# Last stage of a ViT layer: sums kept in three buffers of their own, and loads issued in front of stores

## Chip, cores and metric

One core of a Trainium2 chip. The metric is the device time of one launch in microseconds (us), the median of several runs. In names of the text a number in brackets is a block or a chunk: combine(23), low(29).

## What is computed

A patch embedding, a long convolution along the tokens and a mixture-of-experts layer over 64 images of 197 tokens with 192 channels. What matters here is the end of the last line:

```python
gates, idx = jax.lax.top_k(probs, TOPK_ROUTED)        # 2 of 8 experts
routed = jnp.einsum('bse,bsed->bsd', dense_g, expert_out)
shared = jax.nn.silu(x @ ws_gate) * (x @ ws_up) @ ws_down
return alpha * shared + (1.0 - alpha) * routed         # and h + this
```

For each token the result is a residual row plus `alpha` times the shared expert's row, plus one row from each of its two experts. The latter two rows ("parts") were scattered to DRAM by the stage before.

## The kernel before

The 12,608 tokens are 25 blocks (`NBLK`) of 512, the last one with 384. An earlier stage computes the shared expert of blocks 0 to 19 (`NOW` = 20); the routed experts follow; `finish` (from L1888) is the last stage, and the only one the change touches. It does two things side by side:

- **The shared expert of blocks 20 to 24**, in 30 chunks c = 0 to 29, six for a block (128 of 768 hidden columns each). PE does `up(c)` (gate and up products, L1969), then `down(c - 2)` (L1986). ACT applies SiLU (L2004) and casts the hidden values to `hh` (L2011). DVE does `hidden(c)` (L2029, one input in PSUM, the other in SBUF) and `low(c - 1)` (L2035, `hl` = `hf` minus `hh`, both inputs in SBUF). After a block's last chunk DVE adds PE's rows to `sums` (`token_out`, L2042).
- **The final sum and store of all 25 blocks.** SP loads the two parts of a block into `y[b % 5]` (`load(b)`, L1934); POOL adds them (L2019); DVE adds the block's `sums` (`combine(b)`, L2057, in place in `y`); SP stores the result to the images (`store(b)`, L1945).

Each engine works its list in order. DVE's list is written in the loop at the end of `vector`: in chunk c it issues hidden(c), low(c - 1), after each sixth chunk token_out, and from c = 6 on combine(c - 6). combine(23) falls into the last chunk; low(29), the last token_out and combine(24) follow. So whatever combine(b) waits for also holds hidden(b + 7), behind it, and with it ACT and PE.

SP's list is the loop in `sync`. `RING` = 5 buffers `y`, but `BEHIND` = 3: ahead of load(b) stands store(b - 3), which waits until combine(b - 3) is done, and load(b) itself waits until store(b - 5), the one that emptied its buffer, has landed. `xt` is a ring of 8 buffers (`XR`) with transposed rows for PE, 1,536 values of 16 bits per partition each; the last stage reads those of blocks 20 to 24, which are `xt[4]` to `xt[7]` and `xt[0]`.

Of the kernel before, what the change touches and what calls it, by code (L numbers as in the profile page):

```python
# [14 lines left out]
F32 = mybir.dt.float32  # L15
F16 = mybir.dt.float16
U32 = mybir.dt.uint32
ALU = mybir.AluOpType
ACT = mybir.ActivationFunctionType

B, C, IMG, P = 64, 3, 224, 16
# [4 lines left out]
D = 192  # L26
# [34 lines left out]
BT, NT = 512, 4  # L61
LAST_NT = 3
NBLK = NTOK // BT + 1
CLASS_TILE = LAST_NT - 1
# [21 lines left out]
NOW = NBLK - NLATE  # L86
PACE = [5, 5, 4] * ((NBLK - 1) // 3) + [8]
XR = 8
# [118 lines left out]
def embed(nc, io, outer, u, area, taps, pairs, resid, cls, consts, early_in, corners, row_out, yc, uc, k0, spare, weights):  # L207

    with ExitStack() as ctx:
# [318 lines left out]
        def vector(dve):  # L528
# [193 lines left out]
            for at in range(NG + 2):  # L722
                if 0 < at < NG:
                    fold(at)
                    if at % QG == 0:
                        low_rows(at // QG)
                chain(at)
                if 0 <= at - 2:
                    finish(at - 2)
# [173 lines left out]
def feed_forward(nc, io, embedded, mixing, sums, row_out, weights, resid, cls, routed, parts, out, consts):  # L903

    with ExitStack() as ctx:
# [11 lines left out]
        shared = shared_expert(nc, io, ctx, sems, t, mixing, row_out, weights, resid, cls, routed, out, consts)  # L917
        experts = routed_experts(nc, ctx, sems, t, weights, routed, parts)
        end = finish(nc, ctx, sems, t, weights, parts, out)
        block = ctx.enter_context(nc.Block())  # L920

# [45 lines left out]
def tiles(b):  # L967
    return NT if b < NBLK - 1 else LAST_NT if b == NBLK - 1 else 0


def shared_weights(t):

    w = t["w"]
    wa = [x[:, 0:2 * HS].rearrange("p (k h) -> p k h", k=2) for x in w]
    wb = [x[:, 2 * HS:4 * HS].rearrange("p (k h) -> p k h", k=2) for x in w]
    wd = [x[:, 4 * HS:W_SHARED].rearrange("p (m d) -> p m d", m=NSH) for x in w]
    return wa, wb, wd


def patch_tiles(b):  # L980
    return NT if b < NBLK - 1 else CLASS_TILE


def tile_sums(t, b, i):

    if b == NBLK - 1 and i == CLASS_TILE:
        return halves(t["class"][:])
    at = (b * NT + i) * DH
    return t["sums"][:, :, at:at + DH]


def block_sums(t, b):

    at = b * NT * DH
    return t["sums"][:, :, at:at + patch_tiles(b) * DH].rearrange("p k (t d) -> p k t d", d=DH)


def halves(row):
    return row.rearrange("p (k d) -> p k d", k=2)


def tile_halves(rows):
    return rows.rearrange("p t (k d) -> p k t d", k=2)
# [877 lines left out]
def finish(nc, outer, sems, t, weights, parts, out):  # L1881

    with ExitStack() as ctx:
        def sb(name, shape, dt=F32):
            return ctx.enter_context(nc.sbuf_tensor("end_" + name, shape, dt))

        def sem(name):
            return outer.enter_context(nc.semaphore("e_" + name))  # L1888

        RING, BEHIND = 5, 3  # L1890
        wa, wb, wd = shared_weights(t)
        xt, alpha = t["xt"], t["alpha"]
        y = [sb(f"part{i}", [128, 2, NT, D]) for i in range(3)]
        sb("gap", [128, 584])
        sg = [weights["stage"][0][:, i * BT:(i + 1) * BT] for i in range(2)]
        hf = [weights["stage"][1][:, i * BT:(i + 1) * BT] for i in range(2)]
        hh = [sb(f"hh{i}", [128, BT], F16) for i in range(2)]
# [4 lines left out]
        ctx.enter_context(nc.psum_tensor("end_unused", [128, 2, 512], F32))  # L1902
        pso = ctx.enter_context(nc.psum_tensor("end_out", [128, 2, 512], F32))
        y_in = [sem(f"y_in{i}") for i in range(RING)]
        stored = [sem(f"stored{i}") for i in range(BEHIND)]
        pair_added, all_added = sem("pair_added"), sem("all_added")
        g_ps, u_ps, sg_ready, hf_ready, hh_ready, hl_ready, down_ps, out_ready = (
            sems[n] for n in ("g_ps", "u_ps", "sg_ready", "hf_ready", "hh_ready", "hl_ready", "down", "out_ready"))
# [4 lines left out]
        def place(c):  # L1913

            j, m = divmod(c, NSH)
            return NOW + j, m, tiles(NOW + j)

        LAST = NBLK - 1
        CLASS_ROW = LAST * BT + CLASS_TILE * 128

        def sync(sp, rounds):
            for q in range(RL):
                sp.wait_ge(sems[f"r_sent{q}"], 64 * rounds + 64 * (STRAIGHT // RY))
            sp.wait_ge(sems["r_turn"], 64 * rounds + 64 * (STRAIGHT // RY))
            for q in range(RL, RY):
                sp.wait_ge(sems[f"r_sent{q}"], 64 * (STRAIGHT // RY))

            images = out[0:NTOK].rearrange("(b l) d -> b l d", l=SEQ)

            def load(b):  # L1930
                i, n = b % RING, patch_tiles(b)
                for k in range(2):
                    at = k * NTOK + b * BT
                    sp.dma_start(y[i][:, k, 0:n], parts[at:at + n * 128].rearrange("(p t) d -> p t d", t=n)  # L1934
                                 ).then_inc(y_in[i], 16)
                    if b == LAST:
                        at = k * NTOK + CLASS_ROW
                        sp.dma_start(y[i][0:B, k, CLASS_TILE], parts[at:at + B]).then_inc(y_in[i], 16)

            def store(b):  # L1940
                sp.wait_ge(all_added, b + 1)
                i, n = b % RING, patch_tiles(b)
                for half in range(2):
                    at = 1 + half * HALF + b * NT
                    sp.dma_start(images[:, at:at + n], y[i][half * B:(half + 1) * B, 0, 0:n]).then_inc(stored[b % BEHIND], 16)  # L1945
                if b == LAST:
                    sp.dma_start(images[:, 0], y[i][0:B, 0, CLASS_TILE]).then_inc(stored[b % BEHIND], 16)

            for b in range(NBLK):
                if b >= BEHIND:  # L1950
                    store(b - BEHIND)
                if b >= RING:
                    sp.wait_ge(stored[(b - RING) % BEHIND], 32 * ((b - RING) // BEHIND + 1))
                load(b)
            for b in range(NBLK - BEHIND, NBLK):
                store(b)
            for i in range(BEHIND):
                sp.wait_ge(stored[i], 32 * len(range(i, NBLK, BEHIND)) + (16 if i == LAST % BEHIND else 0))

        def tensor(pe, rounds):  # L1960
            def up(c):
# [60 lines left out]
        def vector(dve):  # L2022
            def hidden(c):
                i, n = c % 2, place(c)[2] * 128
                dve.wait_ge(sg_ready, DONE + c + 1)
                dve.wait_ge(u_ps, DONE + c + 1)
                if c >= 2:
                    dve.wait_ge(hl_ready, DONE + c - 1)
                nc.vector.scalar_tensor_tensor(out=hf[i][:, 0:n], in0=psu[:, i, 0:n], scalar=1.0 / SCALE,  # L2029
                                               in1=sg[i][:, 0:n], op0=ALU.mult, op1=ALU.mult).then_inc(hf_ready, 1)  # L2030

            def low(c):
                i, n = c % 2, place(c)[2] * 128
                dve.wait_ge(hh_ready, DONE + c + 1)
                nc.vector.tensor_tensor(hl[i][:, 0:n], hf[i][:, 0:n], hh[i][:, 0:n],  # L2035
                                        ALU.subtract).then_inc(hl_ready, 1)

            def token_out(b):
                dve.wait_ge(down_ps, NSH * (b + 1))
                for i in range(tiles(b)):  # L2040
                    sums = tile_sums(t, b, i)
                    last = nc.vector.scalar_tensor_tensor(  # L2042
                        out=sums, in0=halves(pso[:, i // 2, (i % 2) * D:(i % 2 + 1) * D]),
                        scalar=alpha[b % XR][:, i:i + 1], in1=sums, op0=ALU.mult, op1=ALU.add)
                    if i % 2 or i == tiles(b) - 1:
                        last.then_inc(out_ready, 1)

            def combine(b):
                i = b % RING
                dve.wait_ge(pair_added, b + 1)  # L2050
                if b >= NOW:
                    dve.wait_ge(out_ready, 2 * (b + 1))
                n = patch_tiles(b)
                if b == LAST:
                    nc.vector.tensor_tensor(y[i][0:B, 0, n], t["class"][0:B], y[i][0:B, 0, n], ALU.add)
                total = tile_halves(y[i][:, 0, 0:n])
                nc.vector.tensor_tensor(total, block_sums(t, b), total, ALU.add).then_inc(all_added, 1)  # L2057

            done = 0
            for c in range(CHUNKS):  # L2060
                hidden(c)
                if c:
                    low(c - 1)
                if c % NSH == 1 and c > NSH:
                    token_out(NOW + c // NSH - 1)
                while done < c + 1 - FIRST_COMBINED:
                    combine(done)
                    done += 1
            low(CHUNKS - 1)
            token_out(NBLK - 1)  # L2070
            for b in range(done, NBLK):
                combine(b)

        return {"sync": sync, "tensor": tensor, "scalar": scalar, "gpsimd": gpsimd, "vector": vector}


# [138 lines left out]
```

## Time and profile before

| what | us |
|---|---|
| median of 3 runs | 1130.31 (1129.49 to 1130.46) |
| the profiled execution's own time | 1131.53 |
| its span in the trace | 1129.5 |
| last stage, from PE's first product (L1969) to the end of the span | 1006.5 to 1129.5 |

The span is what the trace's clock covers; times inside it count from its start. The profiled execution took 1131.53 us, of which 2.0 us lie outside the span. The stages before 1006 us are the same code before and after the change. Start from a DVE row, see what its bracket says it idled for, and go from there to POOL's and SP's rows.

### The profile page before, as it was taken

Reading aid. Unit: us, or ns where it says so; the run is one execution under the profiler, and the core shown is the slowest. Engines: PE = TensorE matmul, PEld = TensorE weight load, DVE = VectorE, ACT = ScalarE, POOL = GpSimd, SP = SyncE. Lnnn points to the kernel's source line nnn. Section 1 sums busy time; section 2 is a strip of 40 time slices with the busy share of each in tenths; the row PEclk is TensorE's granted clock in tenths of the full one; section 3 lists DMA queues with packets and bytes.
Section 4 is the critical chain, followed back from the end, with each engine's and each line's share of the span. In section 5 each row is a group of like instructions: output and inputs, shape, how many; then the busy total and the mean of one; then the engine's idle time right before and its main releaser. Section 6 shows DMA issues by size and latency. Waiting matters only on the chain.

```text
span 1129.5 us, 24252 instructions
## 1 busy us (share of the span) xinstructions
PE 1022.7 (91%) x7867; PEld 715.8 (63%) x7868; DVE 890.9 (79%) x2663; ACT 557.7 (49%) x1047; POOL 630.2 (56%) x637
## 2 busy tenths in 40 slices
PE   5969899599499999999999999899999999989884
PEld 4968788589366666666666666556666656656452
DVE  6999967567688888988888886678888888866885
ACT  1134534357655565565555555246565656543231
POOL 0134521200367777777777786237777777773453
PEclk9999999789699999999999999999999999999898
DMA  9596687866422323332222233747676767616896
GB/s 330 201 306 214 203 284 238 194 173 164 122 72 65 117 69 118 115 96 88 73 82 68 70 105 118 217 96 156 146 163 139 160 146 165 148 66 219 293 316 212
DMA packets 192772, 178.64 MB, mean 158 GB/s; under 512 B 127050, under 2 KB 156942, under 8 KB 192650
## 3 DMA queue, kind: packets, MB, share of 16 engines
q1 hardware_dynamic: 158402, 127.47, 41.3%
q0 software_dynamic: 19488, 39.17, 9.9%
q10 hardware_dynamic: 14760, 10.46, 2.9%
q8 instruction: 67, 1.10, 0.4%
q14 instruction: 55, 0.45, 0.1%
HBM read 90.78 MB, written 66.93 MB: 140 GB/s over the span
## 4 chain that ended last, share of the span: by engine, by line
PE 44%; POOL 19%; DVE 16%; issue 15%; DMA 3%; ACT 1%; SPq 1%; POOLq 0%; ACTq 0%; DVEq 0%
POOL routed L1378 13%; PE u_out L1747 7%; PE ps L514 6%; PE u_gate L1731 5%; PE u_short L1731 5%; PE u_up L1731 5%; PE conv L816 4%; DMA end_part<-parts 3%; DVE u L538 2%; POOL rs L1354 2%; DVE sums L644 2%; PE psg L1212 2%; PE conv L820 2%; PE pso L1227 2%; PE psu L1212 2%
## 5 line engine op out<-in xcount | busy, mean ns | idle before, releaser
L1807 POOL DMA_INDIRECT parts<-unit_yu,unit_token x208 | 204.6, 984 | 89.7 <-issue 49.4
L1378 POOL DMA_INDIRECT routed<-rows_w,slot x198 | 215.1, 1086 | 64.6 <-issue 64.3
L514 PE MATMUL ps<-w,sums 128*98 128x192 f32 x768 | 148.0, 338 | 5.2 <-DVE sums L644 5.2
L1559 DVE SCALAR_TENSOR_TENSOR hf<-psu,sg 128x512 f32<-128x512 f32 x120 | 82.8, 690 | 66.2 <-PE psu L1212 42.5
L1299 ACT ACTIVATE sg<-psg 128x512 f32<-128x512 f32 x120 | 71.9, 599 | 126.8 <-PE psg L1212 126.7
L1227 PE MATMUL pso<-ffn_w_hi,hh 128*128 128x192 f16 x480 | 119.0, 248 | 13.0 <-DVE hl L1564 9.9
L514 PEld LDWEIGHTS ps<-w,sums 128*98 128x98 f32 x768 | 121.9, 170 | 13.3 <-DVE sums L644 5.5
L445 POOL TENSOR_TENSOR e_rs<-e_ve,mhalf 98x8 f32<-98x8 f32 x16 | 50.5, 3154 | 140.0 <-DVE e_ve L681 133.2
L1227 PE MATMUL pso<-ffn_w_hi,hl 128*128 128x192 f16 x480 | 119.0, 248 | 0.0
L1227 PE MATMUL pso<-ffn_w_lo,hh 128*128 128x192 f16 x480 | 118.9, 248 | 0.0
L1212 PE MATMUL psg<-xt,ffn_w_hi 128*128 128x512 f16 x360 | 118.2, 383 | 0.0
L1212 PE MATMUL psu<-xt,ffn_w_hi 128*128 128x512 f16 x360 | 117.2, 380 | 0.0
L393 ACT ACTIVATE u<-sums,e_nb,e_rs 98x192 f32<-98x192 f32 x124 | 56.1, 534 | 90.7 <-POOL e_nb L447 82.1
L1212 PE MATMUL psg<-xt,ffn_w_lo 128*128 128x512 f16 x240 | 91.8, 382 | 0.0
L1212 PE MATMUL psu<-xt,ffn_w_lo 128*128 128x512 f16 x240 | 91.2, 380 | 0.0
L1564 DVE TENSOR_TENSOR hl<-hf,hh 128x512 f16<-128x512 f32 x120 | 90.9, 758 | 0.3 <-ACT hh L1305 0.3
L1772 ACT ACTIVATE unit_yu<-u_out,unit_gates 128x192 f32<-128x192 f32 x104 | 38.1, 418 | 86.2 <-DVE unit_gates L1842 83.3
L1305 ACT CAST hh<-hf 128x512 f16<-128x512 f32 x120 | 73.6, 614 | 8.1 <-DVE hf L1559 7.1
L2019 POOL TENSOR_TENSOR end_part<-end_part 128x768 f32<-128x768 f32 (+1 forms) x25 | 47.9, 1917 | 52.3 <-DMA end_part<-parts 52.3
L1227 PEld LDWEIGHTS pso<-ffn_w_hi,hh 128*128 128x128 f16 x480 | 47.2, 98 | 28.3 <-DVE hl L1564 16.9
L1212 PEld LDWEIGHTS psu<-xt,ffn_w_hi 128*128 128x128 f16 x360 | 35.4, 98 | 43.0 <-issue 0.8
L1860 DVE SCALAR_TENSOR_TENSOR unit_h<-u_up,stage 128x512 f32<-128x512 f32 x52 | 35.9, 691 | 30.2 <-ACT stage L1778 26.9
(236 smaller groups left out, 2768.9 us busy)
## 6 DMA issues: line engine op xcount, KB each, us to landing
sums<-in_xa_dram SPq DMA_DIRECT2D x48, 392.0 KB, 5.5
sums<-in_xb_dram SPq DMA_DIRECT2D x48, 392.0 KB, 6.9
end_part<-parts SPq DMA_DIRECT2D x48, 384.0 KB, 5.1
resid<-sums ACTq DMA_DIRECT2D x32, 294.0 KB
hin<-resid SPq DMA_DIRECT2D x48, 192.0 KB, 3.8
out_dram<-end_part SPq DMA_DIRECT2D x48, 192.0 KB, 3.6
stage<-in_w_all_dram SPq DMA_DIRECT2D x8, 576.0 KB, 4.2
routed<-stage SPq DMA_DIRECT2D x11, 392.0 KB, 5.7
```

Of the source, the lines that this page charges most:

```text
L393: last = nc.scalar.activation(u[0:HALF, n % 2, GI * g + n // 2], h[g % NH][:, n // 2, n % 2], ACT.Identity, bias=nb[g % NH][:, n], scale=r ...
L514: nc.tensor.matmul(out, xa[(C * g + c) % NSLOT][:, t], w32[:, c], start=(plain and c == 0 and k == 0), stop=False, skip_group_check=True)
L1212: last = nc.tensor.matmul(ps[:, m % 2], wt[:, k, cols], xt[b % XR][:, x], start=(a == 0), stop=(a == 4))
L1227: last = nc.tensor.matmul(o, hx[m % 2][:, ts], wd[k][:, m], start=(a == 0 and m == 0 and t % 2 == 0), stop=(a == 2 and m == NSH - 1), skip ...
L1299: nc.scalar.activation(sg[c % 2][:], psg[:, c % 2], ACT.Silu, scale=1.0 / SCALE).then_inc(s["sg_ready"], 1)
L1305: nc.scalar.copy(hh[c % 2][:], hf[c % 2][:]).then_inc(s["hh_ready"], 1)
L1378: nc.gpsimd.indirect_dma_start(out=routed[:, :], out_offset=bass.IndirectOffsetOnAxis(ap=slot[q][:, k, t:t + 1], axis=0), in_=rows_w[q][:, ...
L1559: nc.vector.scalar_tensor_tensor(out=hf[i][:], in0=psu[:, i], scalar=1.0 / SCALE, in1=sg[i][:], op0=ALU.mult, op1=ALU.mult).then_inc(s["hf ...
L1564: nc.vector.tensor_tensor(hl[c % 2][:], hf[c % 2][:], hh[c % 2][:], ALU.subtract).then_inc(s["hl_ready"], 1)
L1731: last = nc.tensor.matmul(ps[:], w[part][:, bass.ds(col + off, 128)], x[:, c], start=(m == 0), stop=(m == 4))
L1747: last = nc.tensor.matmul(o, h[q][:, k * 128:(k + 1) * 128], w[part][:, bass.ds(col + off, D)], start=(m == 0 and k % 2 == 0), stop=(m == ...
L1807: nc.gpsimd.indirect_dma_start(out=parts[:, :], out_offset=bass.IndirectOffsetOnAxis(ap=token[r][:, k:k + 1], axis=0), in_=y[r][:, k, :], ...
```

## The change

```diff
-        RING, BEHIND = 5, 3
+        RING, OUT = 5, 3
+        total = [t["xt"][b % XR][:].rearrange("p c n -> p (c n)").bitcast(F32)[:, 0:NT * D].rearrange("p (t d) -> p t d", t=NT)
+                 for b in range(NOW - OUT, NOW)]
...
             def store(b):
-                sp.wait_ge(all_added, b + 1)
-                i, n = b % RING, patch_tiles(b)
+                i, n = b % OUT, patch_tiles(b)
                 for half in range(2):
                     at = 1 + half * HALF + b * NT
-                    sp.dma_start(images[:, at:at + n], y[i][half * B:(half + 1) * B, 0, 0:n]).then_inc(stored[b % BEHIND], 16)
+                    sp.dma_start(images[:, at:at + n], total[i][half * B:(half + 1) * B, 0:n]).then_inc(stored[i], 16)
...
-            for b in range(NBLK):
-                if b >= BEHIND:
-                    store(b - BEHIND)
+            for b in range(NBLK + RING):
                 if b >= RING:
-                    sp.wait_ge(stored[(b - RING) % BEHIND], 32 * ((b - RING) // BEHIND + 1))
-                load(b)
-            for b in range(NBLK - BEHIND, NBLK):
-                store(b)
+                    sp.wait_ge(all_added, b - RING + 1)
+                if b < NBLK:
+                    load(b)
+                if b >= RING:
+                    store(b - RING)
...
-                n = patch_tiles(b)
+                n, o = patch_tiles(b), total[b % OUT]
+                if b >= OUT:
+                    dve.wait_ge(stored[b % OUT], 32 * (b // OUT))
                 if b == LAST:
-                    nc.vector.tensor_tensor(y[i][0:B, 0, n], t["class"][0:B], y[i][0:B, 0, n], ALU.add)
-                total = tile_halves(y[i][:, 0, 0:n])
-                nc.vector.tensor_tensor(total, block_sums(t, b), total, ALU.add).then_inc(all_added, 1)
+                    nc.vector.tensor_tensor(o[0:B, n], t["class"][0:B], y[i][0:B, 0, n], ALU.add)
+                nc.vector.tensor_tensor(tile_halves(o[:, 0:n]), block_sums(t, b), tile_halves(y[i][:, 0, 0:n]),
+                                        ALU.add).then_inc(all_added, 1)
```

combine(b) now reads `y[b % 5]` and writes `total[b % 3]`, which is `xt[1]`, `xt[2]` or `xt[3]`, last read for blocks 17 to 19. `y[b % 5]` is free once combine(b) is done; the new wait on DVE is for store(b - 3) to have landed, since it reads the same `total`. Sizes and counts of all operations stay.

SP, from the first load of the last stage on. `end_part` is `y`, `xt` is `total`, `out_dram` the images; L1934 (before) and L1936 (changed) are loads, L1945 and L1946 stores. Before:

```order
L1934 DMA end_part<-parts 128x768 [waits r_turn,r_sent3,r_sent4,r_sent2,r_sent5,r_sent1,r_sent0]
L1934 DMA end_part<-parts 128x768 x5
L1945 DMA out_dram<-end_part 64x768 [waits e_all_added]
L1945 DMA out_dram<-end_part 64x768
L1934 DMA end_part<-parts 128x768 x2
L1945 DMA out_dram<-end_part 64x768 [waits e_all_added]
L1945 DMA out_dram<-end_part 64x768
L1934 DMA end_part<-parts 128x768 x2
L1945 DMA out_dram<-end_part 64x768 [waits e_all_added]
L1945 DMA out_dram<-end_part 64x768
L1934 DMA end_part<-parts 128x768 [waits e_stored0]
L1934 DMA end_part<-parts 128x768
```

Changed:

```order
L1936 DMA end_part<-parts 128x768 [waits r_turn,r_sent3,r_sent4,r_sent2,r_sent5,r_sent1,r_sent0]
L1936 DMA end_part<-parts 128x768 x9
L1936 DMA end_part<-parts 128x768 [waits e_all_added]
L1936 DMA end_part<-parts 128x768
L1946 DMA out_dram<-xt 64x768 x2
L1936 DMA end_part<-parts 128x768 [waits e_all_added]
L1936 DMA end_part<-parts 128x768
L1946 DMA out_dram<-xt 64x768 x2
```

Ten loads (five blocks) in place of six go out at once, and a block's stores stand behind the load of the block five later.

DVE, two chunks in the middle of the stage, before:

```order
L2029 SCALAR_TENSOR_TENSOR stage<-end_up,stage 128x512 [waits hl_ready,u_ps,sg_ready]
L2035 TENSOR_TENSOR end_hl<-stage,end_hh 128x512 [waits hh_ready]
L2057 TENSOR_TENSOR end_part<-sums,end_part 128x2x4x96 [waits e_pair_added]
L2029 SCALAR_TENSOR_TENSOR stage<-end_up,stage 128x512 [waits hl_ready,u_ps,sg_ready]
L2035 TENSOR_TENSOR end_hl<-stage,end_hh 128x512 [waits hh_ready]
```

Changed:

```order
L2029 SCALAR_TENSOR_TENSOR stage<-end_up,stage 128x512 [waits hl_ready,u_ps,sg_ready]
L2035 TENSOR_TENSOR end_hl<-stage,end_hh 128x512 [waits hh_ready]
L2058 TENSOR_TENSOR xt<-sums,end_part 128x2x4x96 [waits e_stored2,e_pair_added]
L2029 SCALAR_TENSOR_TENSOR stage<-end_up,stage 128x512 [waits hl_ready,u_ps,sg_ready]
L2035 TENSOR_TENSOR end_hl<-stage,end_hh 128x512 [waits hh_ready]
```

The order of DVE's work is the same; from combine(3) on, combine has one wait more (`e_stored`).

## Rows read from the trace of the kernel before

**Rows 1.** The chain that ended last, 1096 to 1130 us: start, us, what.

```profile
1096.07 0.88 DVE end_part L2057
...
1096.96 0.47 SPq L1945
...
1097.48 0.60 SPq L1945
...
1098.12 0.58 SPq L1934
...
1098.75 6.22 DMA end_part<-parts
...
1105.04 1.82 POOL end_part L2019
...
1106.88 0.97 DVE end_part L2057
```

**Rows 2.** Waits of 1000 to 1130 us: total us, times, longest.

```profile
POOL end_part L2019 <- DMA end_part<-parts: 52.3, 23, 6.5
...
DVE stage L2029 <- PE end_up L1969: 16.2, 10, 2.8
DVE end_part L2057 <- POOL end_part L2019: 12.7, 6, 3.2
```

**Rows 3.** DVE in order of time: start, us, instruction, idle before it.

```profile
1015.19 0.68 DVE L2035 TENSOR_TENSOR end_hl<-stage,end_hh 128x512 f16<-128x512 f32 x1
...
1027.17 0.69 DVE L2029 SCALAR_TENSOR_TENSOR stage<-end_up,stage 128x512 f32<-128x512 f32 x1 [1.86 <-PE end_up L1969]
...
1028.38 2.56 DVE L2057 TENSOR_TENSOR end_part<-sums,end_part 128x768 f32<-128x768 f32 x1
...
1036.46 0.94 DVE L2057 TENSOR_TENSOR end_part<-sums,end_part 128x768 f32<-128x768 f32 x1
...
1050.39 1.69 DVE L2035 TENSOR_TENSOR end_hl<-stage,end_hh 128x512 f16<-128x512 f32 x1
...
1068.37 1.50 DVE L2035 TENSOR_TENSOR end_hl<-stage,end_hh 128x512 f16<-128x512 f32 x1
...
1100.42 0.54 DVE L2035 TENSOR_TENSOR end_hl<-stage,end_hh 128x384 f16<-128x384 f32 x1
...
1117.66 0.96 DVE L2057 TENSOR_TENSOR end_part<-sums,end_part 128x768 f32<-128x768 f32 x1 [2.71 <-POOL end_part L2019]
1118.54 1.89 DVE L2035 TENSOR_TENSOR end_hl<-stage,end_hh 128x384 f16<-128x384 f32 x1
```

**Rows 4.** POOL in order of time, the same columns.

```profile
1049.52 2.02 POOL L2019 TENSOR_TENSOR end_part<-end_part 128x768 f32<-128x768 f32 x1 [1.07 <-DMA end_part<-parts]
...
1093.72 1.80 POOL L2019 TENSOR_TENSOR end_part<-end_part 128x768 f32<-128x768 f32 x1 [1.36 <-DMA end_part<-parts]
```

**Rows 5.** DVE by group and shape, 1004 to 1130 us: xcount | busy us, mean ns | idle.

```profile
L2035 DVE TENSOR_TENSOR end_hl<-stage,end_hh 128x512 f16<-128x512 f32 x24 | 31.3, 1305 | 0.0
L2057 DVE TENSOR_TENSOR end_part<-sums,end_part 128x768 f32<-128x768 f32 x24 | 25.9, 1079 | 12.7 <-POOL end_part L2019 12.7
...
L2035 DVE TENSOR_TENSOR end_hl<-stage,end_hh 128x384 f16<-128x384 f32 x6 | 7.2, 1199 | 0.0
```

**Rows 6.** Windows: busy by engine, granted clock, DMA share, GB/s.

```profile
1030.00:1033.00 3.00, 3.00 (x24) 1.87 (x21) 3.00 (x3) 0.95 (x3) 2.62 (x2) 1.00 0.30 60
1060.00:1063.00 3.00, 0.87 (x7) 0.38 (x6) 3.00 (x4) 0.70 (x2) 1.80 (x1) 1.00 0.62 143
...
1051.00:1054.00 3.00, 3.00 (x10) 1.11 (x9) 1.95 (x2) 1.10 (x2) 0.55 (x2) 0.56 0.95 311
...
1075.00:1115.00 40.00, 31.86 (x230) 19.74 (x228) 34.89 (x43) 11.78 (x23) 21.32 (x11) 1.00 0.96 321
```

**Rows 7.** DMA issues of 1005 to 1130 us: KB each, median us to landing.

```profile
end_part<-parts SPq DMA_DIRECT2D x48, 384.0 KB, 5.1
out_dram<-end_part SPq DMA_DIRECT2D x48, 192.0 KB, 3.6
...
out_dram<-end_part SPq DMA_DIRECT2D x1, 48.0 KB, 2.0
```

**Rows 8.** All stores (L1945): duration of the issue, and us to landing.

```profile
DMA to landing us min/median/max: 2.1/3.5/6.5
```

More of the change, by code:

```diff
@@ L1904, in finish @@
         y_in = [sem(f"y_in{i}") for i in range(RING)]
-        stored = [sem(f"stored{i}") for i in range(BEHIND)]
+        stored = [sem(f"stored{i}") for i in range(OUT)]
         pair_added, all_added = sem("pair_added"), sem("all_added")
@@ L1940, in store @@
             def store(b):
-                sp.wait_ge(all_added, b + 1)
-                i, n = b % RING, patch_tiles(b)
+                i, n = b % OUT, patch_tiles(b)
                 for half in range(2):
                     at = 1 + half * HALF + b * NT
-                    sp.dma_start(images[:, at:at + n], y[i][half * B:(half + 1) * B, 0, 0:n]).then_inc(stored[b % BEHIND], 16)
+                    sp.dma_start(images[:, at:at + n], total[i][half * B:(half + 1) * B, 0:n]).then_inc(stored[i], 16)
                 if b == LAST:
-                    sp.dma_start(images[:, 0], y[i][0:B, 0, CLASS_TILE]).then_inc(stored[b % BEHIND], 16)
-            for b in range(NBLK):
-                if b >= BEHIND:
-                    store(b - BEHIND)
+                    sp.dma_start(images[:, 0], total[i][0:B, CLASS_TILE]).then_inc(stored[i], 16)
+            for b in range(NBLK + RING):
                 if b >= RING:
-                    sp.wait_ge(stored[(b - RING) % BEHIND], 32 * ((b - RING) // BEHIND + 1))
-                load(b)
-            for b in range(NBLK - BEHIND, NBLK):
-                store(b)
-            for i in range(BEHIND):
-                sp.wait_ge(stored[i], 32 * len(range(i, NBLK, BEHIND)) + (16 if i == LAST % BEHIND else 0))
+                    sp.wait_ge(all_added, b - RING + 1)
[3 more added lines that the diff above has]
+                    store(b - RING)
+            for i in range(OUT):
+                sp.wait_ge(stored[i], 32 * len(range(i, NBLK, OUT)) + (16 if i == LAST % OUT else 0))
         def tensor(pe, rounds):
```

## Prediction

> **What bounds the last stage.** The chain that ended last comes first, since every other stage is untouched. At 1096 to 1107 us it reads [rows 1]: combine, two store issues, one load issue, 6.22 us of load, POOL's add, combine. So it walks round a loop: combine(b) is done, SP issues store(b), behind it load(b + 3), and that load is what combine(b + 3) waits for. The list of waits gives the size [rows 2]: DVE idled 12.7 us in 6 waits of combine for POOL's add, and POOL had waited for loads. Ten waits of hidden for PE cost 16.2 us. Those up to 1027.17 us (2.84, 1.47, 0.83 and four of 1.86, in DVE's rows in order of time; the last is in [rows 3]) lie ahead of the first combine and sum to 12.6; the 3.6 left follow such stalls. The granted clock shows why: PE stood still behind a waiting DVE, and 1051 to 1054 us was granted 0.56, mostly the lower level of 1.2 GHz, where most of the stage has 1.00, which is 2.4 GHz [rows 6].
>
> From the start of combine(0), 1028.38, to the end of combine(23), 1118.54 [rows 3], are 90.2 us. DVE idled 12.7 + 3.6 = 16.3 of them and was occupied for the rest. It is the engine that sets the end; from combine(23) to the end of the span is a tail of 11.0 us.
>
> Part of DVE's occupied time is no work. A low takes 0.68 us alone and 1.69 at 1050.39, where POOL's add ran from 1049.52 to 1051.54 [rows 3, 4]: it ends 0.5 us behind POOL's add. By groups [rows 5], with 0.68, 0.54 and 0.94 as the times alone [rows 3], this costs 31.3 - 24 x 0.68 = 15.0, 7.2 - 6 x 0.54 = 4.0 and 25.9 - 24 x 0.94 = 3.3, together 22.3 us. DVE's rows in order of time hold 16 lows over 1.4 us and 2 combines over 2.4: 18 of POOL's 25 adds, 22.3 / 18 = **1.24 us for each add that meets DVE**. The other seven are block 0's and the six for which DVE was waiting idle.
>
> The DMA engines are the third bound, and close: from 1075 to 1115 us they were busy 0.96 at 321 GB/s [rows 6], but earlier there were holes (0.30 at 1030 to 1033, 0.62 at 1060 to 1063).
>
> **The change, part by part.**
>
> *Loads leave two combines earlier.* load(b) waited, through the store ahead of it, for combine(b - 3); now for combine(b - 5). Two chunks are 2 x (90.2 / 23) = 7.8 us, and DVE's longest wait for POOL is 3.2 [rows 2], so all six waits can go: **-12.7 us**. With them go the stalls of PE and what followed them at 1.2 GHz: **-3.6 us**.
>
> *POOL's adds meet DVE.* Six adds ran while DVE stood idle. Now DVE is at work then, so each costs what the others do: 6 x 1.24 = **+7.4 us**. The add of block 24 met low(29) in the tail (1.89 against 0.54 [rows 3], 1.35 us); its load now follows combine(19), so it meets an earlier instruction: 1.35 less in the tail, 1.24 more ahead of it, nothing in the sum. From 0.8 us, the least of the 18 (the low of 1.50 at 1068.37 [rows 3]), to the whole length of an add, 1.80 [rows 4], the six are worth 4.9 to 10.8.
>
> Here a rule speaks against the change. The Trainium skill's page "SBUF — State Buffer" (Who interferes with whom) says that a DVE instruction with two SBUF inputs and a GpSimd instruction that reads SBUF exclude each other for the whole instruction, the loser blocking fully. The trace agrees: the low at 1050.39 ends only after POOL's add has, and hidden, with one input in SBUF, keeps its 0.69. What it would make of an add that always blocks from its start is the second rival below.
>
> *The new wait for store(b - 3).* It can only bite if that store takes longer than three chunks. Between the end of combine(b - 3) and the start of combine(b) lie about 3 x 3.5 - 0.9 = 9.6 us (3.5 is 90.2 less the net 8.9 gained so far, over 23). Before the store stand two load issues (2 x 0.60), then its own two; landing took 3.5 us in the median and 6.5 at most [rows 8]. That is 2.4 + 3.5 to 6.5 = 5.9 to 8.9: hidden, but narrowly, and I cost it at nothing. Its cover is the 0.7 us between 8.9 and 9.6. If the load that now stands ahead of it makes it later by its whole 786 KB, 2.4 us at 321 GB/s, 1.7 are left over in every third combine: 8 x 1.7 = 13.6, the upper end; the lower is zero.
>
> *What the DMA engines allow.* combine(23) needs store(20) landed, and SP asks for all loads ahead of that store: 24 x 786 KB, 492 KB for block 24, and 21 stores of 393 KB (from [rows 7]), 27.6 MB. At the 321 GB/s of the busiest stretch that is 86.0 us, at 321 / 0.96 = 334 it is 82.7. From the first load at 1021.0, with 2.0 us for landing [rows 7] and 0.9 for combine, combine(23) ends no earlier than 1109.9, or 1106.6. DVE's own sum gives 1118.5 - 8.9 = 1109.6. Two bounds meet, and where they do neither is reached. For that meeting no row gives a price. It lies between nothing and 8.9 (all the gain); I take one wait of the size seen now, 12.7 / 6 = **+2.1 us**, near the lower end because the loads have five blocks of slack at the start.
>
> *The rest.* SP issues the same 103 DMAs and drops a wait on its queue; its issue time lies beside DVE's. combine into another buffer has the same shapes, and I cost it at nothing; its cover is DVE's alone, so 0.1 us more for each would add 2.4.
>
> Sum: -12.7 - 3.6 + 7.4 + 2.1 = **-6.8 us**. The profiled execution took 1131.53 and would take 1124.7, its span 1122.7. It lies 1.2 above the median of the runs, 1130.31, from which the forecast is **1123.5 us**. A measurement of this kernel can tell 0.2%, 2.3 us, from no change.
>
> **Rivals.**
>
> *A. The DMA engines set the pace, and fill no better than before.* For it: 0.96 busy already at the end, and the same bytes. Against: holes of 0.30 and 0.62 earlier, with bytes waiting to be asked for. If the mean rate from 1021 on is only 309 GB/s, between the 321 seen and the 298 at which nothing is left, 27.6 MB take 89.3 us and combine(23) ends at 1113.2; with the 2.1 of meeting, 1115.3: a gain of 3.2, **1127.1 us**.
>
> *B. The port takes it back, and more.* The mechanism is POOL's add against low and combine. Adds now start when a load lands, unrelated to where DVE is, and no add finds DVE idle. If each of the 24 costs its whole 1.80, that is 43.2 against 22.3: +20.9 - 16.3 = +4.6, **1134.9 us**, slower. The point is (16.3 + 22.3) / 24 = 1.61 us for an add. For it: two combines took 1.6 extra each (2.56 against 0.94 [rows 3]). Against: the mean is 1.24, since hidden and token_out run beside POOL. At 1.5 the gain would be 2.6 and the time 1127.7.
>
> *C. The new wait replaces the old one.* store(b - 3) behind load(b + 2) lands too late, 1.7 us in every third combine, with DVE held as before: -16.3 + 7.4 + 13.6 = +4.7 at the worst, half of that about the same as now, **1130 us**. Against: while DVE waits no new load is asked for, so the queue drains.
>
> *D. A larger gain.* The six adds cost the least seen, 0.8 each, and no meeting is paid: -16.3 + 4.9 = -11.4, which the DMA bound of 1106.6 (-11.9) just allows; **1118.9 us**.
>
> **From these to the numbers.** Forecast 0.60 (1121 to 1126), D 0.10, A 0.12, B 0.08 of which half is slower than before, C 0.10 split between no change and slower. The range of 8 in 10 leaves out the end of D below and the worst of B and C above: 1119.5 to 1129.0. Faster: 0.60 + 0.10 + most of A and a quarter of B, 0.82. Slower: 0.04 of B and 0.02 of C, 0.06. Same: 0.12.
>
> **What the changed profile would show.** DVE's idle time before combine for POOL near zero, with two or three waits left, the chain's loop of load, POOL and combine gone from most of the stage and DVE, POOL and PE in its place; lows and combines together 28 to 31 us above their times alone, not 22; DMA share 0.95 and more from 1030 us on without holes; end of combine(23) near 1111.7. I am wrong if combine idles for stores (C: `out_dram` as what ended its waits), if the extra of lows and combines is over 36 us (B), or if loads still end POOL's and DVE's waits with the DMA share at 0.95 throughout (A).

## Result and profile after

| | before | changed |
|---|---|---|
| median, us | 1130.38 (4 runs, 1129.49 to 1131.78) | 1123.02 (4 runs, 1121.24 to 1123.41) |
| profiled execution: span | 1129.5 | 1121.4 |
| its last stage, from the first product of L1969 | 1006.5 to 1129.5: 123.0 | 1013.0 to 1121.4: 108.4 |

The ratio is 0.9924 (95% interval 0.9900 to 0.9949): 7.4 us faster in the medians, where 6.8 were forecast. The last row says that this agreement is partly luck. The last stage gained 14.6 us, twice the forecast, and began 6.5 us later, in code that is the same. Some executions fall in a slower state of the chip (three of them took 1750 to 3263 us): the medians, here and in the table of the experiments, are of all runs, the ratios leave such runs out.

The waits of 1000 to 1130 us of the changed kernel, to be read against [rows 2]:

```profile
POOL end_part L2019 <- DMA end_part<-parts: 36.0, 21, 6.8
...
DVE stage L2029 <- PE end_up L1969: 12.4, 9, 2.6
...
DVE xt L2058 <- DMA out_dram<-xt: 0.9, 2, 0.5
```

DVE's 12.7 us of waiting for POOL are gone altogether. In their place stand two waits for stores, 0.9 us. Of the waits for PE, 1.1 us lie behind combine(0), where 3.6 did.

DVE by group and shape, 1004 to 1130 us, against [rows 5]:

```profile
L2035 DVE TENSOR_TENSOR end_hl<-stage,end_hh 128x512 f16<-128x512 f32 x24 | 33.2, 1385 | 0.0
L2058 DVE TENSOR_TENSOR xt<-sums,end_part 128x768 f32<-128x768 f32 x24 | 28.3, 1180 | 0.9 <-DMA out_dram<-xt 0.9
...
L2035 DVE TENSOR_TENSOR end_hl<-stage,end_hh 128x384 f16<-128x384 f32 x6 | 6.7, 1121 | 0.0
```

With the same times alone as before (0.68, 0.94, 0.54) the meetings with POOL's add cost 16.9 + 5.7 + 3.5 = 26.1 us against 22.3. The instructions of combine itself are no dearer for writing elsewhere: 0.94 us where no add is near.

DVE in order of time, the first combine and the end, against [rows 3]:

```profile
1034.14 1.91 DVE L2035 TENSOR_TENSOR end_hl<-stage,end_hh 128x512 f16<-128x512 f32 x1
1035.98 2.56 DVE L2058 TENSOR_TENSOR xt<-sums,end_part 128x768 f32<-128x768 f32 x1
...
1074.94 1.94 DVE L2058 TENSOR_TENSOR xt<-sums,end_part 128x768 f32<-128x768 f32 x1 [0.55 <-DMA out_dram<-xt]
...
1113.35 0.95 DVE L2058 TENSOR_TENSOR xt<-sums,end_part 128x768 f32<-128x768 f32 x1
1114.21 0.55 DVE L2035 TENSOR_TENSOR end_hl<-stage,end_hh 128x384 f16<-128x384 f32 x1
1115.78 0.74 DVE L2042 SCALAR_TENSOR_TENSOR sums<-end_out,alpha,sums 128x192 f32<-128x192 f32 x2 [1.01 <-PE end_out L1986]
```

From the start of combine(0), 1036.0, to the end of combine(23), 1114.2, are 78.2 us, 12.0 less than before. The way from the stage's first product to combine(0) takes 1.1 more (the adds of the first two blocks meet two lows ahead of it, and the second of these, 1.91 us in place of 0.68, delays it), and the tail 7.2 instead of 10.9. In sum +1.1 - 12.0 - 3.7 = -14.6.

Windows over the combines, first of the changed kernel, then of the kernel before:

```profile
1036.00:1114.00 78.00, 69.63 (x494) 42.68 (x493) 76.00 (x87) 24.38 (x47) 46.93 (x24) 1.00 0.92 321
```

```profile
1028.00:1118.00 90.00, 74.84 (x504) 44.44 (x502) 73.66 (x87) 25.29 (x47) 44.88 (x23) 0.96 0.89 293
```

DVE is busy for 76.0 of 78 us, where it was for 73.7 of 90, and the granted clock is 1.00, where it was 0.96.

### The profile page after: what moved, and what is told of

Read it like the earlier page. It is cut to its first block and busy times, and to the rows that moved or that the text cites. A ratio compares the mean times of both kernels' runs of the same rounds, so it can differ in the third digit from the quotient of the medians.

```text
span 1121.4 us, 24269 instructions
## 1 busy us (share of the span) xinstructions
PE 1024.3 (91%) x7867; PEld 717.8 (64%) x7868; DVE 895.0 (80%) x2663; ACT 557.3 (50%) x1047; POOL 633.6 (57%) x637
## 5 line engine op out<-in xcount | busy, mean ns | idle before, releaser
L514 PE MATMUL ps<-w,sums 128*98 128x192 f32 x768 | 151.1, 342 | 3.5 <-DVE sums L644 3.5
L514 PEld LDWEIGHTS ps<-w,sums 128*98 128x98 f32 x768 | 124.2, 173 | 12.3 <-DVE sums L644 3.8
L2019 POOL TENSOR_TENSOR end_part<-end_part 128x768 f32<-128x768 f32 (+1 forms) x25 | 49.7, 1993 | 36.1 <-DMA end_part<-parts 36.0
L1227 PEld LDWEIGHTS pso<-ffn_w_hi,hh 128*128 128x128 f16 x480 | 47.1, 98 | 28.1 <-DVE hl L1564 17.1
```

What stands on the lines that cost most here:

```text
L514: nc.tensor.matmul(out, xa[(C * g + c) % NSLOT][:, t], w32[:, c], start=(plain and c == 0 and k == 0), stop=False, skip_group_check=True)
L1227: last = nc.tensor.matmul(o, hx[m % 2][:, ts], wd[k][:, m], start=(a == 0 and m == 0 and t % 2 == 0), stop=(a == 2 and m == NSH - 1), skip ...
L2019: nc.gpsimd.tensor_tensor(y[i][:, 0, 0:n], y[i][:, 0, 0:n], y[i][:, 1, 0:n], ALU.add).then_inc(pair_added, 1)
```

## Experiments

"Stage" is the time from the first product of L1969 to the end of the span in the run's profile, "combines" that from the start of combine(0) to the end of combine(23). Runs of one group (those with the same figure under "before there") had one chip.

| run | median, us | before there | ratio (95%) | stage | combines | tail |
|---|---|---|---|---|---|---|
| e2 changed | 1258.96 | 1271.47 | 0.9882 (0.9828 to 0.9937) | 111.1 | 81.2 | 7.1 |
| e3 own buffers, old order | 1275.56 | 1271.47 | 1.0025 (0.9974 to 1.0075) | 119.2 | 86.8 | 11.0 |
| e4 in place, BEHIND = 4 | 1269.10 | 1271.47 | 0.9910 (0.9865 to 0.9955) | 114.5 | 83.5 | 8.8 |
| e5 stores first | 1264.32 | 1271.47 | 0.9958 (0.9923 to 0.9993) | 109.2 | 80.7 | 7.2 |
| e1 before | 1133.26 | 1131.46 | 1.0008 (0.9983 to 1.0033) | 122.3 | 89.0 | 11.4 |
| e2b changed | 1122.31 | 1131.46 | 0.9911 (0.9884 to 0.9938) | 108.1 | 77.9 | 7.2 |
| e6 OUT = 2 | 1135.41 | 1131.46 | 1.0033 (1.0011 to 1.0056) | 126.9 | 97.3 | 7.1 |
| e7 combine a chunk earlier | 1123.34 | 1131.46 | 0.9907 (0.9877 to 0.9936) | 112.6 | 83.4 | 8.9 |
| e8 POOL's add cut | 1110.75 | 1129.49 | 0.9818 (0.9765 to 0.9870) | 98.0 | 70.3 | 7.1 |
| e9 half the loads | 1118.84 | 1129.49 | 0.9888 (0.9839 to 0.9938) | 108.4 | 80.8 | 7.1 |
| e10 before, more waits | 1130.15 | 1129.49 | 0.9999 (0.9973 to 1.0024) | 121.3 | 87.3 | 11.0 |
| e11 OUT = 4 | 1122.55 | 1129.49 | 0.9885 (0.9818 to 0.9951) | 110.5 | 80.2 | 7.2 |

The chip of the first group needed 1271 us for the kernel before: from the first product of the routed experts to that of the last stage it took 394.7 us in e2 (758.6 to 1153.3), elsewhere 271.5. The last stage there is like elsewhere, with a granted clock of 0.97 to 1.00 over the combines, so within this group I compare stages. The profiled stages of the kernel before took 123.0 and 122.3 us, those of the changed kernel 108.4, 111.1 and 108.1: a difference of 3 us between two single profiles says little. In e7 combine(23) stands one chunk earlier, so its "combines" and "tail" are cut at another place.

### e2: the changed kernel again

No edit. Expected:

> The changed kernel once more, unaltered. Theory 1 (the last stage gained about 14 us and the stages ahead of it lost 6 in the profiled execution; both belong to the kernel as built): again 1123 us, first product of L1969 near 1013, last stage near 108 us. Theory 2 (the 6 us ahead of the last stage are chance of that one execution): the last stage again 108 us, but its start anywhere from 1006 to 1013, and so a time anywhere from 1117 to 1124.

The stage took 111.1, 2.7 more than the first time, with 4.7 us of waits for stores in four. Its start says nothing on this chip. The ratio, 0.9882, has an interval (0.9828 to 0.9937) that holds both what 14.6 us less would give in 1130, 0.987, and what 7.4 less give, 0.9935. It cannot tell theory 1 from theory 2.

### e3: own buffers with the old order

```diff
-                if b >= RING:
-                    sp.wait_ge(all_added, b - RING + 1)
+                if b >= OUT:
+                    sp.wait_ge(all_added, b - OUT + 1)
+                    store(b - OUT)
                 if b < NBLK:
                     load(b)
-                if b >= RING:
-                    store(b - RING)
```

> Sums in three buffers of their own, but SP's order as before: store(b - 3), then load(b). Theory 1 (what counts is that a load waits for combine(b - 5), not b - 3): combine still waits some 10 to 13 us for loads; time 1128 to 1131. Rival (what counts is that a load no longer waits for a store to land): most of the gain, 1123 to 1125, and waits for loads under 4 us.

The waits of this run, 1180 to 1268 us:

```profile
POOL end_part L2018 <- DMA end_part<-parts: 47.4, 21, 8.3
...
DVE xt L2057 <- POOL end_part L2018: 15.2, 7, 2.9
```

No gain in the median or the ratio, and 15.2 us of combines that wait for POOL and through it for loads. The stage is 3 to 4 us shorter than in the two profiles of the kernel before, which the ratio does not bear out. So a load that need not wait for a store to land brings little or nothing while it still stands behind combine(b - 3). Theory 1 holds, with somewhat more waiting than its 10 to 13 us.

### e4: one combine earlier, without own buffers

```diff
-        RING, BEHIND = 5, 3
+        RING, BEHIND = 5, 4
```

> The kernel before with BEHIND = 4: sums in place, store(b - 4) and then load(b), which also waits for store(b - 5) to land. Theory 1: a load leaves one combine earlier than before, about 3.5 us, more than the longest wait of 3.2: most waits for loads go, 1124 to 1127. Rival (own buffers are needed): the wait for store(b - 5) to land, issued one combine earlier, is then what binds; no gain, 1129 to 1132.

Stage 114.5 against e3's 119.2 and e2's 111.1; no wait of combine for POOL is left in its list. DVE's combines cost more instead, by meeting adds:

```profile
L2057 DVE TENSOR_TENSOR end_part<-sums,end_part 128x768 f32<-128x768 f32 x24 | 37.9, 1581 | 0.0
```

The ratio, 0.9910 (0.9865 to 0.9955), is a larger gain than the 0.994 to 0.997 that theory 1's 1124 to 1127 stand for, and its interval only touches them. So one digit, with no new memory, brings more than half of the stage's gain (4.7 of the 8.1 us between e3 and e2, in one profile of each), and by the ratios alone it cannot be told from the changed kernel.

### e5: stores in front of loads

```diff
                 if b >= RING:
                     sp.wait_ge(all_added, b - RING + 1)
+                    store(b - RING)
                 if b < NBLK:
                     load(b)
-                if b >= RING:
-                    store(b - RING)
```

> The changed kernel with store(b - 5) in front of load(b). Theory 1 (the order within a pair matters little): loads leave 1.2 us later and stores 0.9 us earlier; loads have slack, so within 1 us of the changed kernel, 1122 to 1124. Rival (loads in front are a part of the gain): combine waits for loads again, 3 us or more in sum, 1125 to 1127.

Stage 109.2 against e2's 111.1, with no wait of combine for loads or for stores. The order inside the pair is no part of the gain. The median is 5.4 us above e2's, with intervals that overlap; in a profile nothing stands for it in the last stage, and I leave it.

### e1 and e2b: both kernels on one chip

> The kernel before once more, unaltered, for its profile beside the next run's on the same chip. Theory 1 (the stages ahead of the last one differ by some us between the two kernels as built): the first product of L1969 comes again about 6 us earlier here than with the changed kernel, and the last stage takes 123 us against 108 to 111. Theory 2 (those us belong to one execution): the difference at the start of the last stage is another one, of either sign, and the last stage again 123 against 108 to 111.

> The changed kernel a third time, for the comparison with the profile of the kernel before on the same chip. Last stage 108 to 111 us. Theory 1 (a fixed shift ahead of the last stage): ratio to before 0.992 to 0.994. Theory 2 (chance): ratio near (1130 - 14.6) / 1130 = 0.987.

The last stages repeat: 122.3 and 108.1. In e1 DVE idled 19.0 us in ten waits for POOL and lost 17.1 in meetings, in the first profile of this kernel 16.3 (12.7 of them for POOL) and 22.3. The split varies and the sum less: 36.1 and 38.6. For the changed kernel it is 28.1 here first, 28.3 in e2b and 31.8 in e2 (4.7 idle, 27.1 in meetings).

The ratio is 0.9911: 9.1 us between the medians for 14.2 in the stage. The starts are 1007.3 and 1010.0. Neither theory fits alone; e10 goes on with it.

### e6: two buffers for sums

```diff
-        RING, OUT = 5, 3
+        RING, OUT = 5, 2
```

> The changed kernel with OUT = 2: combine(b) waits for store(b - 2) to land. Theory (stores land some 7.3 us after their combine: 2.4 of issues ahead and 4.9 to landing; two chunks leave 2 x 3.4 - 0.9 = 5.9): DVE waits for stores at most combines, about 1.4 us in every second one up to all of them, 8 to 16 us in sum, so the gain is mostly gone. Rival (the queue drains while DVE waits, so a store lands in 3.5 and the wait stays under 0.2): within 2 us of the changed kernel.

```profile
DVE xt L2058 <- DMA out_dram<-xt: 21.9, 16, 2.6
```

That row, from the waits of 1036 to 1134 us, is rival C of the prediction made real: 21.9 us in 16 waits, a stage of 126.9 and slower than before (ratio 1.0033). The theory's size was 8 to 16. Its parts were right: in the 16 combines that waited, store(b - 2) had landed 5.4 to 8.3 us after its combine, 7.1 in the median, where I had put 7.3, and a wait was 1.4 us on average, as forecast. What was wrong was the sum: 1.4 us in every second of 22 combines up to all of them are 15 to 31 us, not 8 to 16. With three buffers the same wait is 0.9, 4.7 and 0 us.

### e7: combine one chunk earlier

```diff
-        FIRST_COMBINED = 6
+        FIRST_COMBINED = 5
...
-                while done < c + 1 - FIRST_COMBINED:
+                while done < min(c + 1 - FIRST_COMBINED, NBLK - 1):
```

> The changed kernel with combine(b) one chunk earlier (FIRST_COMBINED = 5, combine(24) still last). Theory (DVE sets the end; in chunk 5 it idles 1.9 us for PE): one combine and one meeting with POOL move into idle time, 1 to 2 us faster than the changed kernel. Rival (the DMA engines set the end): loads go out no earlier in the long run, no difference; or combine(0) waits for the first load, with no difference or a loss of up to 1 us.

No gain: 0.9907 beside e2b's 0.9911, and the stage of the profiled execution is longer, 112.6. combine(0) started 20.2 us into the stage, in e2b 23.0, but the combines took 83.4: 11.1 us of meetings of combines against 2.4, and 2.4 us of waits for stores. The theory falls: a combine moved into idle time at the start did not come back as time at the end, since the meetings behind it rose. Whether that belongs to the order or to this one execution was not tried.

### e8: POOL's add cut to one column

```diff
-                nc.gpsimd.tensor_tensor(y[i][:, 0, 0:n], y[i][:, 0, 0:n], y[i][:, 1, 0:n],
-                                        ALU.add).then_inc(pair_added, 1)
+                nc.gpsimd.tensor_tensor(y[i][:, 0, 0:n, 0:1], y[i][:, 0, 0:n, 0:1], y[i][:, 1, 0:n, 0:1],
+                                        ALU.add).then_inc(pair_added, 1)
```

> The changed kernel with POOL's add cut to one column of 192 of each row (so the second part is missing from the other columns of the output). Loads, stores, DVE's and PE's work stay. Theory (DVE sets the end, and 26 us of its time are meetings with POOL's add): lows fall to 0.68 and combines to 0.94, the meetings go; then the DMA engines are next, with 27.6 MB at the 350 GB/s seen, which lets combine(23) end about 82 us after the first load against 88 now: 4 to 7 us faster than the changed kernel. Rival (the DMA engines already set the end, and the meetings only fill the waiting): same time within 2 us, with DVE idle for POOL or stores by 20 us in place of the meetings.

DVE by group and shape, and one window:

```profile
L2058 DVE TENSOR_TENSOR xt<-sums,end_part 128x768 f32<-128x768 f32 x24 | 22.9, 954 | 3.9 <-DMA out_dram<-xt 3.8
L2029 DVE SCALAR_TENSOR_TENSOR stage<-end_up,stage 128x512 f32<-128x512 f32 x24 | 16.6, 691 | 22.3 <-PE end_up L1969 22.3
L2035 DVE TENSOR_TENSOR end_hl<-stage,end_hh 128x512 f16<-128x512 f32 x24 | 16.4, 683 | 0.0
```

```profile
1030.00:1100.00 70.00, 68.31 (x496) 44.27 (x495) 54.03 (x87) 24.71 (x47) 8.03 (x25) 1.00 0.99 376
```

The meetings are gone: 683 ns for a low instead of 1385, 954 for a combine instead of 1180. The stage takes 98.0, 10.4 us less, more than the 4 to 7 I gave, and PE (68.3 of 70 us) is the next bound. Not all of it is the add's: 7.9 us lie in the combines and 1.2 in the low ahead of combine(0), but 1.2 in PE's first products, which had a granted clock of 1.00 in this profile (1009.7 to 1012.2) and of 0.52 in the changed kernel's (1013.0 to 1015.5). The DMA engines moved 376 GB/s over 70 us. So neither the 321 at a share of 0.96 that I read as their limit [rows 6], nor the 350 of the expectation, is the most they can move.

### e9: half the loads

```diff
-                for k in range(2):
+                for k in range(2 if b < RING or b == LAST else 1):
...
-                pool.wait_ge(y_in[i], 32 * (b // RING + 1) + (32 if b == LAST else 0))
+                pool.wait_ge(y_in[i], 32 + 16 * (b // RING) + (48 if b == LAST else 0))
```

> The changed kernel with the second part loaded only for blocks 0 to 4 and 24 (POOL adds what is left in the buffer, so the output is another; 19 x 393 KB of 29 MB less to move). POOL's add, and its meetings with DVE, stay. Theory (DVE with its meetings sets the end): within 2 us of the changed kernel, DMA share near 0.75. Rival (the DMA engines set the end): 25% fewer bytes, the stage ends where PE and DVE allow, 5 us or more faster.

```profile
1029.00:1109.00 80.00, 69.83 (x494) 42.94 (x492) 76.61 (x86) 25.27 (x47) 49.76 (x25) 1.00 0.72 234
```

With 7.5 MB less, 234 GB/s and a DMA share of 0.72, the stage takes 108.4 us, as with all the loads. (Its combine(0) starts 2.5 us earlier into the stage, for the reasons told of e8; the combines take 80.8 us, within the 77.9 to 81.2 of the changed kernel.) The DMA engines do not set the end of the changed kernel. Nor are the meetings an effect of the DMA traffic: here it is a quarter less and they still cost 24.7 us, in e8 it is denser and they are gone. DVE is busy 76.6 of 80 us, as before the cut. The ratio, 0.9888, is within the interval of e2b's.

### e10: the kernel before, with waits that are always met

```diff
                 n = patch_tiles(b)
+                if b >= 3:
+                    dve.wait_ge(all_added, b - 2)
```

> The kernel before with one more wait in each combine from block 3 on, on DVE's own count of combines, which is always met already. Nothing else moves. Theory (a longer program of DVE shifts what lies ahead of the last stage): first product of L1969 at 1009.5 to 1013.5, where the kernel before has 1006.3 and 1007.2, and 3 us slower in the median. Rival (chance, or something else in the change): 1006 to 1008, no difference to before. Last stage 122 to 123 in both.

The hand-over between the stages, from the start of the last group of products of the routed experts (L1731) to the first product of L1969, in before, in the changed kernel and in e8 (columns as in [rows 6]):

```profile
996.60:1006.50 9.90, 6.53 (x54) 4.68 (x53) 6.77 (x21) 3.78 (x8) 8.01 (x10) 0.97 0.19 73
```

```profile
1002.10:1013.00 10.90, 7.54 (x53) 5.62 (x52) 6.72 (x21) 3.77 (x8) 8.72 (x11) 0.80 0.20 74
```

```profile
1000.20:1009.70 9.50, 6.14 (x53) 4.33 (x52) 6.79 (x21) 3.77 (x8) 7.63 (x10) 1.00 0.20 76
```

The same 53 or 54 products take 9.9 us in before and in e1, but 11.0 in e10 and 10.9 to 11.0 in the changed kernel, e2b, e6, e7 and e11, and 9.5 in e8 and e9. What goes with it is the granted clock: 0.97 in the first two, 0.79 or 0.80 in those with 11, 1.00 in e8 and e9. PE's busy time alone (6.53, 7.54 and 6.14 us in the rows above) makes the difference. So these 1.1 us are PE at 1.2 GHz, a level to which the clock fell earlier in some kernels than in others. That waits in DVE's program cause it is not shown: e10 has it, but e8 and e9, with all the waits of the changed kernel, have not.

The start, 1009.4, is at the edge of what the theory gave, but the median moved by nothing: 0.9999, in an interval from 3.0 us less to 2.7 us more. It leaves out the 3 us that the theory gave. The rest of the difference is older: the first products of L816 start at 221.4 and 222.2 in the two profiles of before, at 223.0 in e10, and at 224.4, 223.2 and 221.7 in the changed kernel, e2b and e7; those of L1731 at 735.0 and 735.8, at 736.8, and at 740.4, 737.4 and 737.9. That part comes and goes between kernels whose program is the same there.

### e11: four buffers for sums

```diff
-        RING, OUT = 5, 3
+        RING, OUT = 5, 4
...
         y += [sb(f"part{i}", [128, 2, NT, D]) for i in range(3, RING)]
+        total.append(sb("more", [128, NT, D])[:])
```

> The changed kernel with OUT = 4: a fourth buffer for sums, in memory of its own. Theory (waits for stores are a small rest: 0.9, 4.7 and 0 us in three profiles): those waits are zero, and the last stage is 107 to 109 us, 0 to 2 us faster than the changed kernel. Rival (what DVE does not wait for stores it waits for loads or POOL, since the DMA engines are at their rate): no difference.

No wait for a store is left, but the stage is 110.5, not the 107 to 109 of the theory; the ratio 0.9885 has an interval that holds e2b's. Three buffers are enough. None of the variants that compute the whole result is shown to beat the changed kernel.

## Why the prediction came out as it did

The forecast, 1123.5 us, lies 0.5 from the result, but its sum of -6.8 was too small for the last stage, and it had no term for what came ahead of it.

- **Loads leave two combines earlier, -12.7 and -3.6.** Right in mechanism, and in size for the first: idle time between combine(0) and combine(23) fell from 16.3 to 2.0 us, and no combine waited for POOL in three profiles. The -3.6 of PE's stalls does not hang on these waits as I wrote. Of it 2.4 us (2.22 at 1067.77 and 0.17 behind it) came 20 us after the last wait for POOL, behind a low that had met an add (1060.57, 2.04 us): PE waited 2.13 us for it and was then granted 0.61 from 1063 to 1067. e1 had 19.0 us of waits for POOL and no such stall, e2b none of the former and 3.4 us of idling for PE. So its fall to 1.1 in the first profile was partly luck. e3 and e4 show that the combine a load waits for is what counts (15.2 us of waits behind combine(b - 3), none behind b - 4), and e5 that the order in the pair is not.
- **POOL's adds meet DVE, +7.4.** Right in kind, too dear. Over the stage the meetings rose from 22.3 to 26.1 us (24.9 in e2b, 27.1 in e2), so +3.8 and not +7.4. Both the number of meetings and their price were put too high: lows and combines lengthened by 0.8 us or more went from 18 to 22, not to 24, and cost 25.1 / 22 = 1.14 us each and not 1.24 (three more, of 0.3 to 0.4, make up the rest). Which adds escaped was not traced. The rule of the Trainium skill's page "SBUF — State Buffer" (Who interferes with whom) holds here, and e8 measured it: with POOL's add cut, both kinds of DVE instruction fell to their times alone, and 9 us of the stage went.
- **What the DMA engines allow, +2.1.** This step failed. I took 321 GB/s at a busy share of 0.96, or 334 at 1.00, for the most they give, and let two bounds meet near 1110 us. e8 ran them at 376 GB/s and e9 showed that a quarter fewer bytes change nothing. At 376 the same 27.6 MB take 73.4 us, 9 below the 82.7 of the prediction. The trace of before held the warning: in the same 40 us from 1075 to 1115, single microseconds with a share of 0.9 or more moved anything from 237 to 406 GB/s. Rival A falls with it.
- **The new wait for store(b - 3), 0.** Right for this kernel: 0.9, 4.7 and 0 us in three profiles. The cover was as thin as said: with one buffer less it costs 21.9 us and the kernel is slower than before.
- **The tail, nothing in the sum.** It is 3.7 us shorter. I saw that low(29) would be free of its add (1.89 to 0.55 us), and set a meeting elsewhere against it; these 1.35 us are in the +3.8 above. What I left out are two more: DVE's wait for the last products (1.71 to 1.01 us, at a granted clock of 0.50 from 1120 to 1123 before and of 1.00 from 1115 to 1117 now) and the time from the last combine to the end (5.4 to 3.7 us). The latter is not a matter of the stores: in both kernels the last of them is issued 1.2 us after that combine and lands 2.0 us later. Then the span goes on for 2.2 us before (4.0 in e1) and 0.5 now. The trace shows nothing in that time, and its cause stays open.
- **"Every other stage is untouched."** As code, yes, but the last stage began 6.5 us later in the first profile of the changed kernel and 2.7 later in the pair e1 and e2b. Of either, about 1.1 us is PE at the lower clock level in the hand-over to the last stage (e10); the rest was neither steady nor explained. What makes unchanged code start later, and the clock fall earlier, stays open.

So -14.6 in the stage, of which 6.8 were forecast. Of the 7.8 us between them, 3.6 are meetings that did not come, 2.1 the DMA term, 2.4 the rest of the tail and 1.3 idling for PE ahead of combine(0) that the lengthened lows took up, less the 2.0 us of idling that stayed; 0.4 is left over. By the medians (7.4 and 9.1 us less, where the stages lost 14.6 and 14.2) 5 to 7 us were given back ahead of it, of which none was forecast: two errors of opposite sign, and it is luck that they nearly cancel. The range of 1119.5 to 1129.0 was wide enough for both. Of the rivals, D was the nearest to what the stage did: combine(23) ended 12.0 - 1.1 = 10.9 us earlier into the stage, where D had 11.4. Of the signs named beforehand, the waits of combine for POOL went (none left, where two or three were expected), the extra of lows and combines is 26.1 us and not 28 to 31, and the DMA share is 0.92 over the combines and not 0.95.

## What to carry to other kernels

In a ring of buffers, find which event a reload really stands behind, through everything that shares its queue, and count how many steps back it lies; moving it one step back (a 4 for a 3) gave more than half of the gain that new buffers gave. A DMA busy share of 0.95 was no ceiling here: take the bytes away, or look for a stretch with more GB/s, before it becomes a bound in a sum. And where time falls by tens of us in one stage, compare that stage's own length in the two profiles, not only the totals, and the granted clock at its start before a difference is booked to an edit.

## What the runs showed of the hardware

- The same DMA issues moved 321 GB/s at a share of 0.92 to 0.96, and 376 at 0.99 once POOL's add was away. Which of the things that changed with it gave the rate was not tried apart.
- DVE's idle time and its meetings with POOL trade against each other: 38.6 and 36.1 us together in two profiles of before, 28.1, 28.3 and 31.8 in three of the changed kernel, while the split moved by 5 us between the two of before.
- Kernels that differ only in the last stage reached its first product at 1006.5 to 1013.5 us on the chips other than that of the first group (there at 1153 to 1159). The same products just ahead of it took 9.5 us at a granted clock of 1.00, 9.9 at 0.97 and 10.9 to 11.0 at 0.79 to 0.80.
